# Retention block between two channel mixes on one core: fp32 operands for block 1's first channel mix and block 0's query, key and value, and a new order of fill and drain

## What is computed

```python
x = x + 0.5 * ffn(layernorm(x))        # first channel mix, "FFN1"
x = x + retention(layernorm(x)) @ Wo   # 8 heads of 32, chunked recurrence, "RET"
x = x + 0.5 * ffn(layernorm(x))        # second channel mix, "FFN2", same weights

def ffn(x):
    x_prev = x shifted by one token, zeros in front
    xr = mu_r * x + (1 - mu_r) * x_prev
    xk = mu_k * x + (1 - mu_k) * x_prev
    return sigmoid(xr @ W_r.T) * (square(relu(xk @ W_k.T)) @ W_v.T)

def retention(x):
    q, k, v = x @ Wq, x @ Wk, x @ Wv          # 8 heads
    # per chunk: o = (q k^T * D) v + (q * decay_q) S;  S = decay_s * S + (k * decay_k)^T v
```

## Time and profile before

| | us |
|---|---|
| median of 3 runs | 336.74 (335.70 to 337.18) |
| the profiled execution's own time | 336.37 |
| its span in the trace | 334.3 |
| PE busy | 323.2 (97%) |
| DVE busy | 297.5 (89%) |
| ACT busy | 208.8 (62%) |
| POOL busy | 136.7 (41%) |
| DMA, share of 16 engines over the span | 10.5% and less per queue |

### The profile page before, as it was taken

The page is one execution under the profiler, slowest core; times in us unless marked ns, Lnnn a source line. Parts: engine busy times, 40 slices in busy tenths (PEclk is TensorE's granted clock), DMA queues, the critical chain, the costliest instruction groups (busy, mean ns, idle before and its releaser), DMA issues.

```text
span 334.3 us, 11299 instructions
## 1 busy us (share of the span) xinstructions
PE 323.2 (97%) x4266; PEld 303.3 (91%) x4266; DVE 297.5 (89%) x698; ACT 208.8 (62%) x417; POOL 136.7 (41%) x242
## 2 busy tenths in 40 slices
PE   7779999999999999999999999999999999999984
PEld 7669999999999999999899999989999999989884
DVE  3999988998999999899999989999997979689973
ACT  3786675775757586575758667575866638275452
POOL 2585373607063450706245170624516244231321
PEclk9999999999999999999999999999999999999999
DMA  7611010101002020100102020011000000000001
GB/s 243 240 35 33 3 31 4 32 4 64 5 3 61 2 66 3 64 4 14 54 2 66 2 64 4 16 50 34 2 2 34 2 33 4 33 2 34 2 31 63
DMA packets 11556, 12.08 MB, mean 36 GB/s; under 512 B 1008, under 2 KB 11120, under 8 KB 11504
## 3 DMA queue, kind: packets, MB, share of 16 engines
q1 hardware_dynamic: 11072, 11.18, 10.5%
q10 hardware_dynamic: 432, 0.20, 0.2%
HBM read 7.18 MB, written 4.19 MB: 34 GB/s over the span
## 4 chain that ended last, share of the span: by engine, by line
PE 89%; DVE 5%; issue 2%; DMA 2%; ACT 1%; SPq 0%; DVEq 0%; ACTq 0%
PE psum L992 39%; PE psum L984 26%; PE psum L976 6%; PE psum L1063 5%; PE psum L1095 5%; PE psum L1082 3%; PE psum L1053 2%; PE psum L1108 2%; DMA x<-in_x 2%; DVE stats L640 1%; DVE xrT L686 1%; DVE dT L666 1%; DVE w_lo L171 1%; PE psum L1189 1%; DVE xkT L677 1%
## 5 line engine op out<-in xcount | busy, mean ns | idle before, releaser
L208 POOL TENSOR_TENSOR xr_lo<-xrT,xr_hi 128x512 fp32r<-128x512 f32 x28 | 46.7, 1681 | 110.6 <-ACT xr_hi L394 110.6
L363 ACT ACTIVATE xn<-x,shift,rstd 128x256 f32<-128x256 f32 x92 | 49.8, 591 | 3.4 <-POOL shift L296 3.3
L722 DVE TENSOR_TENSOR attn<-psum,decay 128x512 f32<-128x512 f32 x64 | 42.1, 683 | 4.7 <-PE psum L1063 4.7
L640 DVE BATCH_NORM_STATS2 stats<-x 128x6 f32<-128x256 f32 x96 | 35.7, 413 | 4.5 <-DMA x<-in_x 4.1
L992 PE MATMUL psum<-w_hi,xr_hi 128*128 128x256 f32 x124 | 38.6, 311 | 1.1 <-DVE w_lo L171 1.1
L433 ACT ACTIVATE kT<-psum 128x512 f32<-128x512 f32 x16 | 9.6, 599 | 46.3 <-PE psum L984 46.2
L292 POOL TENSOR_TENSOR rstd<-var_eps,exponent 128x2 f32<-128x2 f32 x48 | 34.6, 721 | 6.4 <-DVE var_eps L651 6.4
L984 PE MATMUL psum<-xa_hi,w_hi 128*128 128x256 f32 x128 | 36.4, 285 | 0.1
L992 PE MATMUL psum<-w_hi,ka_hi 128*128 128x256 f32 x120 | 35.4, 295 | 0.7 <-ACT rgate L422 0.7
L984 PE MATMUL psum<-xa_hi,w_lo 128*128 128x256 f32 x128 | 35.6, 278 | 0.0
L984 PE MATMUL psum<-xa_lo,w_hi 128*128 128x256 f32 x128 | 35.6, 278 | 0.0
(11 more groups left out here) (107 smaller groups left out, 1041.7 us busy)
## 6 DMA issues: line engine op xcount, KB each, us to landing
x<-in_x SPq DMA_DIRECT2D x15, 256.0 KB, 2.9
x_out<-y SPq DMA_DIRECT2D x15, 256.0 KB, 3.1
w_f<-in_w SPq DMA_DIRECT2D x7, 256.0 KB, 6.4
decay<-in_decay SPq DMA_DIRECT2D x1, 512.0 KB, 6.9
decq<-in_decq SPq DMA_DIRECT2D x1, 256.0 KB, 6.5
deck<-in_deck SPq DMA_DIRECT2D x1, 256.0 KB, 6.6
x_out<-y SPq DMA_DIRECT2D x2, 128.0 KB, 1.8
x<-in_x ACTq DMA_DIRECT2D x1, 128.0 KB, 2.6
```

Source lines behind the costliest of these rows:

```text
L208: engine.tensor_tensor(xr_lo[f][n % 2][:], xrT[f][n % 2][:], xr_hi[f][n % 2][:].bitcast(F32), ALU.subtract).then_inc(xr_lo_ready[f], 1)
L363: act.activation(xn[s][n % 2][:, t, :], x[n % len(x)][:, t, :], ACT.Identity, bias=shift[s][n % 2][:, t:t + 1], scale=rstd[s][n % 2][:, t: ...
L640: dve.bn_stats(stats[s][n % 2][:, t, :], x[n % len(x)][:, t, :]).then_inc(stats_ready[s], 1)
L722: dve.tensor_tensor(attn[r][:], bank[B_SCORES[r]].rearrange("p (g c i) -> p g c i", g=G, c=TILES), decay[:, r, :, :].unsqueeze(2).broadcas ...
```

## The change

Several things change, all in the fill and the drain; the loops are the same but for the counts of one semaphore, `xa_lo_ready`.

- Block 1's first channel mix is no longer split: `hidden_fp32_halves`, `gate_fp32` and `ffn_out_fp32_halves` take its fp32 operands (`UNSPLIT = 2`). Its `xk_high`, `xk_low`, `xr_high`, `xr_low`, `square_high` and `square_low` are gone.
- Block 0's query, key and value take a plain fp32 copy, `xa_first`, and the fp32 weights (`first_T_fp32`, `first_rows_fp32`). `xa_low(0)` is gone; `xa_high(0)` writes `xa_first`.
- With a second unsplit block the split weights are needed later, and their splits stand later in the lists, some on another engine: the high part of W_R and of W_VAL on DVE (before POOL and ACT), the low part of W_R and W_KEY on POOL (before DVE).
- In DVE's fill `layer_stats(FFN1, 2)` stands ahead of the first `difference`, and `split_high` of W_R stands between the halves of block 0's `mix_k`.
- Fill of PE: the transpositions stand between halves of products, and block 0's `scores` ahead of the second half of its value product.
- Drain of all engines: another order from the block 13 on. `gate(FFN2, 14, 1)` stands ahead of `keep_warm`; `xr_low(FFN2, 14)` moves from DVE to POOL, behind `xk_low(FFN2, 14)`; `gate(FFN2, 13, 1)` stands ahead of `inter(15)`.
- Three PSUM banks of the split-in-parts products are others.

```diff
-        B_HID_1, B_OUT_1 = {FFN1: 4, FFN2: 5}, {FFN1: 1, FFN2: 2}
+        B_HID_1, B_OUT_1 = {FFN1: 4, FFN2: 4}, {FFN1: 0, FFN2: 3}
...
+        UNSPLIT = 2
+
         def splits(f, n):
-            return max(n - 1, 0) if f == FFN1 else n
+            return max(n - UNSPLIT, 0) if f == FFN1 else n
...
             def xa_high(n):
                 act.wait_ge(xnT_psum[RET], n + 1)
                 act.wait_ge(val_psum, n)
-                act.activation(xa_hi[:], halves(B_T[RET]), ACT.Copy).then_inc(xa_hi_ready, 1)
+                act.activation(xa_hi[:] if n > 0 else xa_first[:], halves(B_T[RET]), ACT.Copy).then_inc(xa_hi_ready, 1)
...
             inverse_std(FFN1, 0)
-            split_high(pool, W_R)
             inverse_std(FFN1, 1)
+            inverse_std(FFN1, 2)
+            inverse_std(RET, 0)
             split_high(pool, W_Q)
...
             layer_stats(FFN1, 1, x0)
+            layer_stats(FFN1, 2, x0)
             difference(FFN1, 0, part=0)
+            mix_k(FFN1, 0, part=0)
+            split_high(dve, W_R)
             difference(FFN1, 0, part=1)
-            mix_k(FFN1, 0, part=0)
             mix_k(FFN1, 0, part=1)
-            split_low(dve, W_K)
             mix_r(FFN1, 0)
-            split_low(dve, W_V)
-            layer_stats(FFN1, 2, x0)
             difference(FFN1, 1)
             mix_k(FFN1, 1)
             mix_r(FFN1, 1)
-            xk_low(dve, FFN1, 1)
+            split_low(dve, W_V)
             gate(FFN1, 0, part=0)
...
+            def first_T_fp32(b, w, half, done):
+                if half == 0:
+                    pe.wait_ge(xa_hi_ready, 1)
+                    pe.wait_ge(w_loaded[w], 16)
+                cols = slice(half * P, (half + 1) * P)
+                for g in range(G):
+                    mm = pe.matmul(halves(b)[:, half, :], w_f32[w][:, g, cols], xa_first[:, g, :], start=(g == 0), stop=(g == 1))
+                if half == 1:
+                    mm.then_inc(done, 1)
...
+            def hidden_fp32_halves(f, n, half):
+                if half == 0:
+                    pe.wait_ge(xk_ready[f], 2 * n + 2)
+                cols = slice(half * P, (half + 1) * P)
+                for g in range(G):
+                    mm = pe.matmul(halves(B_HID[f])[:, half, :], w_f32[W_K][:, g, cols], xkT[f][n % 2][:, g, :], start=(g == 0), stop=(g == 1))
...
             pe.wait_ge(relu_ready[FFN1], 1)
-            hidden(FFN1, 1, 0)
-            hidden(FFN1, 1, 1)
+            hidden_fp32_halves(FFN1, 1, 0)
             pe.wait_ge(xnT_ready[FFN1], 2)
             transpose_T(FFN1, 2)
+            hidden_fp32_halves(FFN1, 1, 1)
             pe.wait_ge(gate_ready[FFN1], 1)
-            gate(FFN1, 1, 0)
-            gate(FFN1, 1, 1)
+            gate_fp32(FFN1, 1, 0)
+            gate_fp32(FFN1, 1, 1)
             pe.wait_ge(gated[FFN1], 1)
+            ffn_out_fp32_halves(FFN1, 1, 0)
             transpose_T(RET, 0)
+            ffn_out_fp32_halves(FFN1, 1, 1)
...
             gate(FFN2, 14, 0)
+            gate(FFN2, 14, 1)
             pe.wait_ge(xnT_ready[FFN2], 15)
             keep_warm(B_T[FFN2], 16)
             transpose_T(FFN2, 15)
-            gate(FFN2, 14, 1)
```

More of the change, by code:

```diff
@@ L623, in _ @@
             relu(FFN2, 15, part=0)
+            square_high(FFN2, 15, part=0)
+            relu(FFN2, 15, part=1)
             square_act(FFN2, 15, part=0)
-            relu(FFN2, 15, part=1)
-            square_high(FFN2, 15, part=0)
             square_high(FFN2, 15, part=1)
@@ L813, in _ @@
-            xa_low(2)
-            update_state(1, 1)
-            difference(FFN2, 0)
-            mix_k(FFN2, 0)
-            mix_r(FFN1, 4)
-            o_low(1)
-            mix_r(FFN2, 0)
-            xk_low(dve, FFN2, 0)
-            xk_low(dve, FFN1, 4)
-            gate(FFN1, 3)
-            add_retention(1)
-            decayed_query(2)
-            layer_stats(FFN2, 1, x2)
-            add_ffn(dve, FFN1, 3)
+            xk_low(dve, FFN1, 3)
+            o_low(0)
+            xr_low(dve, FFN1, 3)
@@ new lines, in _ @@
+            gate(FFN1, 2)
+            scale_state(0, 1)
+            difference(FFN1, 4)
+            add_retention(0)
+            layer_stats(FFN2, 0, x2)
+            decayed_key(1)
+            layer_stats(RET, 2, x1)
+            update_state(0, 1)
+            mask_scores(1, 1)
+            mask_scores(2, 1)
+            scale_state(1, 1)
+            mask_scores(3, 1)
+            mask_scores(0, 1)
+            layer_stats(FFN1, 5, x0)
+            difference(FFN2, 0)
+            xa_low(2)
@@ L827, in _ @@
+            mix_k(FFN1, 4)
+            o_low(1)
+            mix_k(FFN2, 0)
+            update_state(1, 1)
+            decayed_query(2)
+            add_retention(1)
+            layer_stats(FFN2, 1, x2)
+            gate(FFN1, 3)
+            mix_r(FFN2, 0)
+            add_ffn(dve, FFN1, 3)
+            mix_r(FFN1, 4)
             layer_stats(RET, 3, x1)
+            xr_low(dve, FFN2, 0)
             square(dve, FFN2, 0)
@@ L995, in weight_split @@
             def weight_split(n, w):
-                if n == 0 or (n == 1 and w in (W_R, W_K, W_V)):
+                if (n == 0 and w == W_O) or (n == 1 and w in (W_Q, W_KEY, W_VAL)) or (n <= UNSPLIT and w in (W_R, W_K, W_V)):
                     pe.wait_ge(w_hi_ready[w], 1)
@@ L1422, in _ @@
             pe.wait_ge(xout_ready[RET], 13)
-            scores(13, 0, first=True)
-            scores(13, 3)
-            scores(13, 2)
-            scores(13, 1, last=True)
+            scores(13, 2, first=True)
+            hidden(FFN1, 15, 1)
             pe.wait_ge(state_ready[1], 13)
             key_rows(13)
+            scores(13, 0)
+            scores(13, 1)
+            scores(13, 3, last=True)
             pe.wait_ge(relu_ready[FFN1], 16)
@@ L1444, in _ @@
             ffn_out(FFN2, 11, 0)
+            pe.wait_ge(val_ready, 14)
+            transpose_T(FFN2, 12)
+            ffn_out(FFN1, 15, 1)
+            pe.wait_ge(attn_ready[2], 14)
+            transpose_T(RET, 14)
+            gate(FFN1, 15, 1)
             ffn_out(FFN2, 11, 1)
-            pe.wait_ge(xa_lo_ready, 15)
-            key(14, 0)
             pe.wait_ge(attn_ready[3], 14)
@@ L1522, in _ @@
             transpose_T(FFN2, 14)
+            gate(FFN2, 13, 1)
             pe.wait_ge(attn_ready[3], 16)
@@ L1525, in _ @@
             inter(15, first=True)
-            gate(FFN2, 13, 1)
             intra(15)
```

409 lines of the change are left out of this document (200 added, 209 removed).

## The result

The changed kernel takes **337.52 us** in the median of 10 runs (336.82 to 338.12); the kernel before, on the same chip, 336.42 us (335.70 to 337.18, 10 runs). The ratio is 1.0033 with a 95% interval of 1.0021 to 1.0044: 1.1 us slower, sure in its sign, and within the half per cent that counts as no visible change.

The account below looks back on a forecast made before the run. PE, busy 97% of the span, was taken to bound the kernel. Fill +0.35, drain to block 15's scores +0.6 and on to the last transposition +0.4 raised 336.4 to 337.7, put at a median of 337.8 us, range 335.2 to 339.9.

Parts of the forecast that it names:

- Six conversions: Six split products on PE become fp32, 1.73 us each instead of 1.42: +1.9 us in the fill.
- Start of the fill: Block 2's statistics on DVE, waiting for their load, delay PE's first product to 10.55: +1.0 us, bounds +0.6 to +1.7.
- The cast on DVE: Fill: casting W_R's high part between the halves of `mix_k` takes 0.6 us, bounds 0.3 and 0.7.
- RET's first transposition: Middle of the fill: RET's first tile comes at 22.2, PE's wait grows from 0.8 to 1.15: +0.35 us.
- From there on I find PE with work at each step.: Fill, after RET's first block: PE has no waits up to block 1's scores, low parts coming 1 to 3 us ahead.
- The fill's sum: All fill terms together: +0.35 us, block 1's scores starting at 45.0 against 44.64.
- Drain up to block 15's scores: Gaps at FFN2's block 11 relu (0.3) and RET's block 15 normalization (0.2), a matmul-size change (0.1): +0.6 us.
- Scores to the transposition: Drain, block 15's scores to last transposition: `retention_out(15)` 0.8 sooner, `xk_lo` wait 0.65, gate half ahead of `keep_warm` +0.71; together +0.4 us.
- DVE's list holds up the fill: Rival: block 2 lands with W_V near 9.2, delaying all behind it on DVE; slower, 339.5 us, chance 0.25.
- The waits really close: Rival: block 2, RET's tile, the drain's close places and `xk_lo` are all in time; faster, 334.8 us, chance 0.14.
- The clock falls: Rival: PE's longer idle after warm-up halves the clock, first products take twice their time; 342 us, chance 0.02.
- The parts cancel: Rival: saved splits were never on PE's path and the drain's order only trades places; 336.8 us, chance 0.10.

Follow-up runs that it names:

- The second measurement: The unaltered changed kernel timed again beside the others: 337.86 us against 336.30 for the kernel before, ratio 1.0047.
- the mixed kernels: Two kernels: new fill and loop with old drain, 335.62 us, ratio 0.9993; old fill and loop with new drain, 337.60 us, ratio 1.0055.
- fill_mended: The mended fill: new fill, old drain, block 2's statistics back behind `mix_r`, plus four reorderings on ACT, DVE and POOL; 334.56 us, ratio 0.9947 to before.
- xk_first: Changed kernel with `xk_high(FFN2, 14)` ahead of `xr_high` and the halo on ACT; one run, 336.06 us.
- gate_behind: Changed kernel with `gate(FFN2, 14, 1)` behind the last transposition again; 336.84 us, ratio 1.0036 to the kernel before.
- warm4: Changed kernel with 4 instead of 16 matmuls in `keep_warm`; one run, 336.20 us.
- the spare tile: Kernel before plus one unused 128x512 fp32 SBUF tile where the changed kernel has `xa_first`; 335.79 us, ratio 1.0001.
- the mended drain: Kernel before with selected parts of the new drain and `xk_high` ahead of `xr_high` and halo on ACT; 335.63 us, ratio 0.9979.
- the kernel with both mended parts: The mended fill and the mended drain together; 334.23 us, ratio 0.9943 to the kernel before.

## Why the prediction was right, point by point

The forecast was 337.8 us, +1.06 on the median shown, and 337.52 was measured, +1.1 on the kernel before beside it. That these two differences agree so well is partly luck. The terms themselves add up to +1.35; the forecast added them to a profiled execution 0.4 below the median of three runs, and that median came down by 0.3 with ten. The second measurement had +1.6. And the halves were both off: by the mixed kernels the fill is worth -0.2 us (-0.5 to 0.0) where I had +0.35, and the drain +1.9 (1.4 to 2.2; 1.6 by the two traces) where I had +1.0. Most mechanisms were right, several terms were mis-sized, one was missing, and the errors cancelled.

- **Six conversions, +1.9.** Right: 1.72 us from start to start.
- **Start of the fill, +1.0.** Right in mechanism, and near in size over all executions, though here it was +0.04 (9.58 against 9.54). Block 2's statistics ahead of the first difference tie PE's first product to block 2's landing. Over the six executions with that order, DVE started those statistics between 7.43 and 8.68 and PE started at 9.54 to 10.78, 10.03 in the mean, against 8.87 to 9.54 in the four with the old order, 9.18 in the mean: +0.85. The landing, put at 8.5 from even spacing, was mostly earlier; the latest start seen was 8.68. The 1.1 us from there to the next instruction was a reading slip: the earlier trace rows have 7.10 to 8.12, so 1.0, and 1.05 was measured.
- **The cast on DVE, 0.6.** Wrong: 0.33 us to the next start. I took the nearest rows, other engines' casts. The Trainium skill, "VectorE: DVE Perf Modes", section "The perf-mode tier table", gave the better estimate: a copy at twice the rate of a two-input operation, so 0.3. The trace agrees: 0.33 against 0.60 for the low part's subtraction, to the next start.
- **Block 1's normalized tile, -0.8, and the low part of W_R, -1.3.** Right: neither wait is left.
- **RET's first transposition, tile at 22.2 and a longer wait, +0.35.** Wrong: it starts at 20.29, and the gap ahead of it is 0.24 instead of the 0.8 before, so the term is -0.55. It was 0.24 or 0.25 in all six executions with this fill, whenever PE had started. The tile was there 10.7 us after PE's first product and not 11.65, so I had its chain too long; I named the sigmoid on ACT, and which link was too long was not taken apart.
- **"From there on I find PE with work at each step."** This is the step that failed. PE waited 1.0 us for the decayed query, in every execution of the new fill whose list was not mended. It stood behind `mix_r`, a gate, an addition and a block's statistics on DVE, and I had followed the lists at the lengths that these instructions have undisturbed. Beside POOL's subtractions they were longer: the second half of `mix_r` took 1.50 and not 0.48, the addition 1.26 and not 0.68. With the addition alone at its usual length some 0.4 of the wait would be left, by this trace. The mended fill closes the wait without touching either, by taking the statistics (1.1 us) from ahead of the decayed query; that it would close too with POOL's subtractions elsewhere is argued from the lengths and was not tried.
- **The fill's sum.** The two errors nearly cancel (-0.9 and +1.0). From first product to block 1's scores I had 34.45, and it was 34.6 in every execution with that order, against 34.9 to 35.1 with the old fill. Then 0.3 us more came back up to block 2's scores (17.97 against 18.26), which I had not costed. Together, with the mean start of +0.85, about +0.1 where I had +0.35; the timed runs of the fill alone say -0.2, and +0.1 lies just outside their interval.
- **Drain up to block 15's scores, +0.6.** It was +0.43, and 0.36 between executions with the same pace of the loop (51.85 in the second one against 51.49): right in sign, a little large. Neither place I named shows as a wait: from 250 us to these scores the view of PE's waits lists none, before or now. Where it comes from is open.
- **Scores to the transposition, +0.4.** Measured +1.27. The mechanisms are the four named, and the mis-sized terms are the wait for `xk_lo` (0.65 forecast, 0.86 measured) and the gain of `retention_out`. The low part was forecast for 8.85 after the scores. It was ready at 317.97, 9.45 after them: POOL started 0.15 later than I had it, and took 1.72 and not 1.29. With the hand-over PE went on at 9.6. The 0.8 that `retention_out` was to gain was 0.55 (7.12 us after the scores, 7.67 before, by PE's records), since it now waits 0.3 for `o_lo`; but PE was early for `xk_lo` even so. So the stretch grew by 1.27, and `xk_first` gets 1.1 of it back, `gate_behind` 0.67, `warm4` 1.44: not to be added, since each uncovers the next.
- **The tail, 0.** Right: 12.75 against 12.78 by PE's records, though its waits are spread otherwise.
- **The loop.** Not forecast, +0.47 in this execution, and absent in the second execution of the same kernel.

The rivals. *DVE's list holds up the fill*: its mechanism is real, and one execution went far towards it (statistics at 8.68, first product at 10.78), but its price was too high, since the distance to block 1's scores stayed 34.6: nothing was lost a second time by the cast or the sigmoid. *The waits really close*: not with these lists, but `fill_mended` closes those of the fill, and lands at 334.56. *The clock falls*: it didn't where it would cost. The granted clock stayed at 1.00 even behind 2.17 us of idle PE at the start. But it does fall: in three of the thirteen traced executions, those of the spare tile, of `warm4` and of the mended drain, it is at 0.50 at the very end of the span, behind PE's last matmul. One timed run of the kernel with both mended parts, which has no trace, took 336.52 us at a mean granted clock of 0.995, 2.3 us over the median of its kernel; where its clock fell is not known. *The parts cancel*: true of the fill alone, within its interval; the drain's new order did not merely trade places.

## What to carry to other kernels

Moving an item ahead in an in-order list pays only if the followers on that engine, and on the engines behind it, are put in the order in which the bound engine needs them; the same fill gave nothing with a few items misplaced and 1.6 us with them in place. A saved split on an engine with room is worth the wait it closes, and here each one cost 0.3 us of the bound engine. And before an elementwise instruction is placed on POOL, look at what DVE runs beside it at that time, in both directions: POOL's can come late where PE waits for it, and DVE's, with a chain of PE's behind it, can be held up in turn.

## What the hardware showed that I had not expected

- A DVE addition of two SBUF tiles (128x512, fp32) beside a POOL subtraction: the one issued second stretched, DVE's from 0.68 to 1.26 us, POOL's from 1.29 to 1.72. The second half of a `mix_r` (128x256, two SBUF tiles) went from 0.48 to 1.50 in the same way.
- The granted clock fell to 0.50 behind PE's last matmul, before the span had ended, in three of the thirteen traced executions (mean 0.61 over 332 to 334 us in the mended drain's), and stayed at 1.00 to the end in the other ten. It cost nothing there.
- The first loads land at different times from one execution to the next: statistics of block 2, which wait for the load, started at 7.43 to 8.68 with the same code ahead of them, and the time to block 1's scores followed one for one.
- The loop of PE runs at 19.40 or at 19.455 us a block, by execution and at the same granted clock. Over ten blocks this is half a microsecond, a third of the difference between the two spans. A comparison of single traces must be made stage by stage for this reason. Its cause is open. Open too is whether the six conversions alone, in the old order of the fill, would pay, since that was not tried.
